# An overwritten full-height matmul in front of own-key scores and projections in layer 1's attention

## The chip, the cores and the metric

One NeuronCore of one Trainium2 chip runs the whole program. Its engines are TensorE (PE in the rows; its weight loads are PEld), VectorE (DVE), ScalarE (ACT), GpSimd (POOL) and SyncE, which issues the DMAs. Each engine has its own instruction stream and takes it in order; semaphores order the engines against each other. The metric is the device time of one execution in microseconds, as the median of several.

## The reference

A stack of four layers works on x of shape (8, 256, 128): 8 batches of 256 tokens. Each layer adds a gated attention and a gated FFN to x. The change touches the attention of layer 1 alone, which is this (text has 64 keys per batch, x has 256):

```python
q = x @ Wq.T
k = jnp.concatenate([x_text @ Wk.T, x @ Wk.T], axis=1)
v = jnp.concatenate([x_text @ Wv.T, x @ Wv.T], axis=1)
...                                   # 16 heads of 8 channels
scores = jnp.einsum('bhnd,bhkd->bhnk', q, k) / jnp.sqrt(jnp.float32(d))
first = jnp.tanh(gate) * jnp.ones_like(scores[..., :1])
rest = jax.nn.softmax(scores[..., 1:], axis=-1)
attn = jnp.concatenate([first, rest], axis=-1)
out = jnp.einsum('bhnk,bhkd->bhnd', attn, v)
...                                   # to bfloat16 and back, layer norm
return out @ Wp.T + bp
```

The x that goes in is layer-normalised. Layers 0 and 2 have attention over the 64 text keys only, layer 3 has its own function.

## The kernel before, in words

The program is a sequence of stages: `setup`, then `attention` and `ffn` for layers 0, 1 and 2, `attention3` and `ffn` for layer 3, and `store`. Within a stage each engine has a function that emits its stream; all of them walk the same list of steps, and each takes the steps in which it has a part. Layer 1's attention is `attention(pr, 1, own_keys=True, ...)`. Only this call has own keys.

Its 16 heads are worked on in NG = 4 groups of 4 heads. A head's 8 channels are spread over 32 partitions (hi and lo parts of a float32 beside each other), so that one group fills the 128 partitions. The 8 batches are worked on one after the other, and within a batch the 4 groups. A batch and group has these steps:

- `proj` (L543 to L545): q and k of the group, six matmuls of 128 rows and 256 columns into `b_proj`. ScalarE (L705) and VectorE (L830) bring them to SBUF in two parts.
- `scores` (L559 and L566), NS = 5 of them. Step 0 is against the text keys, with all 4 heads at once (128 rows). Steps 1 to 4 are against the own keys, one head each: two matmuls on a strip of 32 rows. Each step fills a bank of two in turn, `b_sc`, and VectorE reduces it to row maxima (L842, L844).
- `maxima` (L579): the maxima are turned on TensorE; ScalarE and VectorE (L712, L865, L867) make of them and of q the operand `mt`.
- `weights` (L594 and L604), again 5: the transposed scores less the maximum. Step 0 has 128 rows, steps 1 to 4 have 32 rows, on the strip of head i. ScalarE takes the exponential (L718) from one of two banks, `b_st`.
- `pv` (L631), 5 steps for every two groups: 8 matmuls each, 128 rows by 32 columns, of the exponentials with the values.
- per batch: `turn` (L526) transposes the normalised x, `values` (L612) projects v, `o_turn` (L648), `on_turn` (L654) and `y` (L660) turn, normalise and project the output.

The order of the steps is written out by hand in `order(b)`. While the weights of group g are computed, the scores of group g+2 and the projection of group g+3 are issued. A group begins with the first score step of group g+2, the projection of g+3 and the maxima of g+1; then `mixed` interleaves the weights of g, the other score steps of g+2 and the value products: weights 0, scores 1, pv, weights 1, scores 2, pv, weights 2, scores 3, pv (in every other group), weights 3, scores 4, weights 4. In the prediction k counts these rounds from 0. Weights k lie on the row strip of head k-1 and scores k+1 on that of head k, so the two are on different strips for k of 1 to 3.

What holds TensorE in these steps: an own-key score step waits until VectorE has reduced the step two before it (`sc_taken`, from the helper `need`), a weights step until ScalarE has taken the one two before (`exp_done`), a projection until x has been turned (`xt_lo`) and the projection before it has been taken (`qk_split`).

Of the kernel before, what the change touches and what calls it, by code (L numbers as in the profile page):

```python
# [23 lines left out]
P = 128  # L24
# [27 lines left out]
def need(eng, sem, value):  # L52

    if isinstance(value, int) and value <= 0:
        return
    eng.wait_ge(sem, value)
# [117 lines left out]
def attention(pr, layer, own_keys, masked, biased, scale, extra=None):  # L174
# [8 lines left out]
    with nc.cleanup_on_exit(), ExitStack() as scope:  # L183
        def sb(name, shape, dt=F32):
            return scope.enter_context(nc.sbuf_tensor(f"{n}_{name}", shape, dt))

        wf = sb("wf", [P, 4, D]) if gated else None
        wx = sb("wx", [P, 4, NG * P], F32R)
# [70 lines left out]
        b_proj, b_turn, b_sc, b_st, b_mt, b_o = (pr.bank[0], pr.bank[1], pr.bank[2:4], pr.bank[4:6], pr.bank[6], pr.bank[7])  # L259
# [65 lines left out]
        with nc.Block() as block:  # L325
# [152 lines left out]
            def _(pe):  # L478
# [5 lines left out]
                if biased:  # L484

                    pe.wait_ge(sem["prep_dve"], 3)
                    for i in range(2):
                        for g in range(NG):
                            last = pe.matmul(b_sc[1][:, i * NG + g:i * NG + g + 1], bias_x[0:1, i, g * P:(g + 1) * P], ones1[0:1, 0:1],
                                             start=True, stop=True)  # L490
# [9 lines left out]
                for h, bank in enumerate((b_proj, b_turn)):  # L500
                    if biased:
                        pe.matmul(bank[:], ones1[:], bias_row[0:1, 2:3, :].to_broadcast([1, 4, D]), start=True, stop=False, skip_group_check=True)
                    for e in range(4):
                        last = pe.matmul(bank[:, e * D:(e + 1) * D], pr.ctx_t2[:, 4 * h + e].rearrange("p a s -> p (a s)"), w[2],
                                         start=not biased, stop=True, skip_group_check=True)
                    last.then_inc(sem["prep_pe"], 1)
                if gated:

                    for h in range(2):
                        pe.wait_ge(sem["prep_dve"], DVE_READY)  # L510
                        for e in range(4):
                            last = pe.matmul(b_sc[h][:, e * D:(e + 1) * D], pr.ctx_t2[:, 4 * h + e, 0, 0:1].to_broadcast([P, P]), wvg[:],
                                             start=True, stop=True, skip_group_check=True)
# [2 lines left out]
                pe.wait_ge(sem["prep_act"], ACT_READY)  # L516
                pe.wait_ge(sem["prep_pool"], POOL_READY)

                def turn(b):
                    pe.wait_ge(sem["xn_ready"], b + 1)  # L520
                    if own_keys:
                        need(pe, sem["v_ready"], b)
                    need(pe, sem["x_done"], b - 2)
                    need(pe, sem["xt_lo"], b)
                    for t in range(2):
                        last = pe.transpose(b_turn[:, t * P:(t + 1) * P], xn[:, t], pr.id())  # L526
                    last.then_inc(sem["xn_turned"], 1)
# [9 lines left out]
                def proj(b, g):  # L537
                    pe.wait_ge(sem["xt_lo"], b + 1)
                    need(pe, sem["qk_split"], b * NG + g)
                    cols = slice(g * P, (g + 1) * P)  # L540
                    for i in range(2 if own_keys else 1):
                        o = b_proj[:, i * S:(i + 1) * S]
                        pe.matmul(o, wx[:, 2 * i, cols], xt_hi[:], start=True, stop=False)  # L543
                        pe.matmul(o, wx[:, 2 * i, cols], xt_lo[:], start=False, stop=False)
                        last = pe.matmul(o, wx[:, 2 * i + 1, cols], xt_hi[:], start=False, stop=True)  # L545
                    last.then_inc(sem["proj_done"], 1)

                def scores(b, g, i):
                    at = g * NS
                    need(pe, sem["sc_taken"], b * U + (at + i - 1))  # L550
                    o = b_sc[(at + i) % 2]
                    if i == 0:
                        pe.wait_ge(sem["qk_split"], b * NG + g + 1)
                        pe.wait_ge(sem["kc_ready"], b * NG + g + 1)
                        if masked:
                            pe.wait_ge(sem["mk_split"], b + 1)
                        for t in range(2):
                            ts = slice(t * P, (t + 1) * P)
                            last = pe.matmul(o[:, t * S:(t + 1) * S], q[:, g, ts], kc[:, g], start=True, stop=not masked)  # L559
                            if masked:  # L560
                                last = pe.matmul(o[:, t * S:(t + 1) * S], msk[:, ts], i2[:, 0:S2].unsqueeze(1).to_broadcast([P, GH, S2]),
                                                 start=False, stop=True)
                    else:
                        rows = slice(32 * (i - 1), 32 * i)
                        for t in range(2):
                            last = pe.matmul(o[:, t * S:(t + 1) * S], q[rows, g, t * P:(t + 1) * P], k[rows, g], start=True, stop=True)  # L566
                    last.then_inc(sem["sc_done"], 1)
# [89 lines left out]
                def y(b):  # L657
                    pe.wait_ge(sem["o2t_ready"], b + 1)
                    for t in range(2):
                        last = pe.matmul(b_turn[:, t * P:(t + 1) * P], o2t[:, t * P:(t + 1) * P], w[3], start=True, stop=True)  # L660
                    last.then_inc(sem["y_done"], 1)

                passes(pe, {"turn": turn, "mask": mask, "proj": proj, "scores": scores, "maxima": maxima, "weights": weights,
                            "values": values, "pv": pv, "o_turn": o_turn, "on_turn": on_turn, "y": y})

# [1209 lines left out]
```

## Time and profile before

| | us |
|---|---|
| median of 3 runs | 1292.36 |
| lowest and highest | 1283.95, 1293.24 |
| the profiled execution | 1285.64 |
| its span, first to last instruction | 1283.9 |
| TensorE busy in the span | 977.4 |
| VectorE busy | 771.4 |
| ScalarE busy | 571.7 |
| GpSimd busy | 393.6 |

The profile is of one execution. The mean granted clock of TensorE over it was 0.842 of full speed. In the profile's rows a matmul's duration is the time from its start to its modelled end; matmuls overlap, so what one costs is read from the distance between starts.

### The profile page before, as it was taken

What the parts mean: (1) busy time and instruction counts of PE and PEld (TensorE: products, weight loads), DVE (VectorE), ACT (ScalarE), POOL (GpSimd) and SP (SyncE); (2) the same over time, 40 slices, a digit from 0 to 9 for tenths busy, and PEclk for the clock granted to TensorE, in tenths of its full rate; (3) what the DMA queues carried; (4) which work ended last, traced back from release to release, by engine and by line L of the source; (5) the groups of instructions that cost most, each with busy time, mean ns of one, the idle gap of its engine ahead of it and who ended that gap; (6) DMA issues with size and microseconds to landing.
All of it is one profiled execution on the core that took longest, in us unless ns stands there. A gap on an engine that the chain in (4) does not pass through costs nothing. (4 is left out here: it accounts for less than half of the span.)

```text
span 1283.9 us, 17163 instructions
## 1 busy us (share of the span) xinstructions
PE 977.4 (76%) x5366; PEld 731.0 (57%) x5366; DVE 771.4 (60%) x1924; ACT 571.7 (45%) x1101; POOL 393.6 (31%) x519
## 2 busy tenths in 40 slices
PE   2797576698888888488888888478867578883766
PEld 2575354566566665266666666357745357772544
DVE  3687565566766777366666656356765414545674
ACT  1575242355555555155555544156634133321553
POOL 2432002122323232146565656333310132210321
PEclk9899677667777778689999999689978679996887
DMA  4000000000000000000000000100000200000001
GB/s 117 1 2 2 1 1 19 1 18 18 18 18 18 18 9 10 1 1 1 1 1 1 1 1 1 36 1 2 2 19 1 64 2 1 1 1 1 1 1 33
DMA packets 25607, 14.12 MB, mean 11 GB/s; under 512 B 10776, under 2 KB 25007, under 8 KB 25391
## 3 DMA queue, kind: packets, MB, share of 16 engines
q1 hardware_dynamic: 25518, 13.03, 3.8%
q8 instruction: 45, 0.74, 0.2%
q14 instruction: 44, 0.35, 0.1%
HBM read 11.98 MB, written 1.05 MB: 10 GB/s over the span
## 5 line engine op out<-in xcount | busy, mean ns | idle before, releaser
L1470 POOL TENSOR_TENSOR L1f_h<-L1f_h,L1f_gb 128x512 f32<-128x512 f32 (+1 forms) x96 | 152.2, 1588 | 116.5 <-DVE L1f_h L1760 96.7
L718 ACT ACTIVATE L_pt<-bank 128x512 f32<-128x512 f32 x224 | 131.3, 597 | 60.8 <-PE bank L604 56.9
L705 ACT ACTIVATE L_part<-bank,L_bias_ca,const 128x256 fp32r<-128x256 f32 x128 | 68.9, 563 | 111.9 <-PE bank L545 111.9
L406 POOL TENSOR_TENSOR L_kc<-L_kc_all,const 128x256 fp32r<-128x256 f32 x96 | 59.0, 618 | 179.7 <-PE bank L604 127.1
L1760 DVE TENSOR_TENSOR L1f_h<-L1f_a,bank 128x512 f32<-128x512 f32 (+1 forms) x96 | 65.4, 682 | 69.9 <-ACT L1f_a L1600 69.3
L1600 ACT ACTIVATE L1f_a<-bank 128x512 f32<-128x512 f32 (+1 forms) x96 | 57.3, 597 | 111.9 <-PE bank L1525 111.8
L1768 DVE TENSOR_TENSOR L1f_h_lo<-L1f_h,L1f_h_hi 128x512 fp32r<-128x512 f32 (+1 forms) x96 | 88.2, 919 | 11.1 <-ACT L1f_h_hi L1613 11.1
L844 DVE TENSOR_REDUCE L_ms<-bank 128x2 f32<-128x512 f32 x128 | 84.5, 687 | 17.0 <-PE bank L566 16.7
L566 PE MATMUL bank<-L_k,L_q 32*128 32x256 f32 x256 | 73.4, 397 | 12.2 <-DVE L_ms L844 8.9
L830 DVE SCALAR_TENSOR_TENSOR L_q<-bank,L_bias_c,L_part 128x256 fp32r<-128x256 f32 x96 | 46.2, 481 | 58.9 <-ACT L_part L705 57.7
L842 DVE TENSOR_REDUCE L_mc<-bank 128x8 f32<-128x512 f32 (+1 forms) x96 | 65.4, 682 | 24.2 <-PE bank L559 14.8
L1523 PE MATMUL bank<-L1f_xt_hi,big_hi 128*128 128x512 f32 (+1 forms) x192 | 77.6, 404 | 0.0
L1524 PE MATMUL bank<-L1f_xt_lo,big_hi 128*128 128x512 f32 (+1 forms) x192 | 76.6, 399 | 0.0
L1525 PE MATMUL bank<-L1f_xt_hi,big_lo 128*128 128x512 f32 (+1 forms) x192 | 76.4, 398 | 0.0
L604 PEld LDWEIGHTS bank<-L_mt,L_k 32*128 32x128 f32 x256 | 45.2, 228 | 43.9 <-ACT L_pt L718 25.3
L604 PE MATMUL bank<-L_mt,L_k 32*128 32x256 f32 x256 | 66.9, 365 | 2.1 <-ACT L_pt L718 2.1
L543 PE MATMUL bank<-L_xt_hi,L_wx 128*128 128x256 f32 x128 | 46.8, 366 | 24.5 <-DVE L_xt_lo L817 18.6
L1545 PE MATMUL bank<-L1f_h_hi,big_hi 128*128 128x512 f32 (+1 forms) x96 | 41.4, 431 | 30.0 <-DVE L1f_h_lo L1768 29.7
L559 PE MATMUL bank<-L_kc,L_q 128*128 128x256 f32 x192 | 56.9, 362 | 8.5 <-DVE L_msk L824 5.2
L1613 ACT CAST L1f_h_hi<-L1f_h 128x512 fp32r<-128x512 f32 (+1 forms) x96 | 59.0, 615 | 2.1 <-POOL L1f_h L1470 2.1
L566 PEld LDWEIGHTS bank<-L_k,L_q 32*128 32x128 f32 x256 | 45.0, 235 | 24.3 <-DVE L_ms L844 13.9
L631 PE MATMUL bank<-L_pt,L_vs 128*32 128x256 f32 x512 | 48.8, 465 | 0.0
(405 smaller groups left out, 2608.9 us busy)
## 6 DMA issues: line engine op xcount, KB each, us to landing
L_raw<-in_L_ffn_w_dram SPq DMA_DIRECT2D x8, 176.0 KB, 2.3
L_raw<-in_L_ffn_v_dram SPq DMA_DIRECT2D x8, 176.0 KB, 2.5
const<-in_const_dram SPq DMA_DIRECT2D x1, 1036.0 KB, 5.0
x<-in_x_dram SPq DMA_DIRECT2D x2, 512.0 KB
L_raw<-in_L_ffn_w_dram SPq DMA_DIRECT2D x8, 128.0 KB, 2.6
L_mask<-in_mask_Bx1xSxS_ff_dram SPq DMA_DIRECT2D x2, 512.0 KB
out_dram<-x SPq DMA_DIRECT2D x2, 512.0 KB
L_raw<-in_L_ffn_w_dram SPq DMA_DIRECT2D x8, 48.0 KB, 2.5
```

The lines of the kernel that those rows point to most:

```text
L566: last = pe.matmul(o[:, t * S:(t + 1) * S], q[rows, g, t * P:(t + 1) * P], k[rows, g], start=True, stop=True)
L604: last = pe.matmul(op, k[rows, g, kt * P:(kt + 1) * P], mt[rows, g % 2], start=True, stop=True)
L705: last = act.activation(part[:, i].bitcast(F32R), b_proj[:, i * S:(i + 1) * S], ACT.Identity, bias=bias_ca[:, i, g:g + 1], scale=pr.c("ak" ...
L718: act.activation(pt[:, g // 2, (g % 2) * NS + i], b_st[(g * NS + i) % 2][:], ACT.Exp, scale=scale).then_inc(sem["exp_done"], 1)
L842: dve.tensor_reduce(mc[:].rearrange("p t j -> p (t j)"), by_head[:, :, start:], AX_X, ALU.max).then_inc(sem["sc_taken"], 1)
L844: dve.tensor_reduce(ms[:, :, i - 1], bank.rearrange("p (t s) -> p t s", s=S), AX_X, ALU.max).then_inc(sem["sc_taken"], 1)
L1470: pool.tensor_tensor(h[0:m, r], h[0:m, r], gb[0:m, gate_slot(c)], ALU.mult).then_inc(sem["h_done"], 1)
L1523: pe.matmul(bank[0:m], hi[:, at:at + m], xh, start=True, stop=False)
L1524: pe.matmul(bank[0:m], hi[:, at:at + m], xl, start=False, stop=False)
L1525: last = pe.matmul(bank[0:m], lo[:, at:at + m], xh, start=False, stop=True)
L1760: dve.tensor_tensor(h[0:m, r], a[0:m, r], b_u[c % NS][0:m], ALU.mult).then_inc(sem["half_done"], 1)
L1768: dve.tensor_tensor(h_lo[0:m, r], h[0:m, r], h_hi[0:m, r].bitcast(F32), ALU.subtract).then_inc(sem["lo_done"], 1)
```

## The change

In TensorE's stream of the attention a helper is added which issues one matmul: the first 128 columns of `wx[:, 0]` as weights (128 rows, 128 columns) and `wx[:, 1]` as the moving operand (512 columns), start and stop set, into a whole bank. It is called with `b_proj` after the waits of a projection and before its first matmul, and with the score bank `o` in front of the two matmuls of each own-key score step. The matmuls that follow write the same columns with start set, so the result is overwritten. Both calls are made only where the layer has own keys, which is layer 1: 32 projections and 128 score steps. No semaphore, wait or other engine is touched.

```diff
@@ -516,6 +516,10 @@
                 pe.wait_ge(sem["prep_act"], ACT_READY)
                 pe.wait_ge(sem["prep_pool"], POOL_READY)
 
+                def keep_clock(bank):
+
+                    pe.matmul(bank[:], wx[:, 0, 0:P], wx[:, 1], start=True, stop=True)
+
                 def turn(b):
                     pe.wait_ge(sem["xn_ready"], b + 1)
                     if own_keys:
@@ -538,6 +542,8 @@
                     pe.wait_ge(sem["xt_lo"], b + 1)
                     need(pe, sem["qk_split"], b * NG + g)
                     cols = slice(g * P, (g + 1) * P)
+                    if own_keys:
+                        keep_clock(b_proj)
                     for i in range(2 if own_keys else 1):
                         o = b_proj[:, i * S:(i + 1) * S]
                         pe.matmul(o, wx[:, 2 * i, cols], xt_hi[:], start=True, stop=False)
@@ -561,6 +567,7 @@
                                 last = pe.matmul(o[:, t * S:(t + 1) * S], msk[:, ts], i2[:, 0:S2].unsqueeze(1).to_broadcast([P, GH, S2]),
                                                  start=False, stop=True)
                     else:
+                        keep_clock(o)
                         rows = slice(32 * (i - 1), 32 * i)
                         for t in range(2):
                             last = pe.matmul(o[:, t * S:(t + 1) * S], q[rows, g, t * P:(t + 1) * P], k[rows, g], start=True, stop=True)
```

## Rows read from the trace of the kernel before

**Rows 1.** The page: span, and TensorE's granted clock in 40 slices.

```profile
span 1283.9 us, 17163 instructions
...
PEclk9899677667777778689999999689978679996887
```

**Rows 2.** Windows: busy PE, PEld, DVE, ACT, POOL; PEclk, DMA share, GB/s.

```profile
225.00:530.00 305.00, 257.85 (x1677) 178.42 (x1677) 200.76 (x426) 155.01 (x309) 79.00 (x168) 0.73 0.05 13
397.10:433.40 36.30, 31.98 (x209) 22.29 (x209) 25.02 (x54) 18.95 (x38) 9.85 (x21) 0.73 0.06 15
399.00:405.00 6.00, 5.75 (x35) 3.13 (x34) 4.05 (x8) 3.71 (x8) 1.81 (x8) 0.50 0.00 0
497.00:503.00 6.00, 5.47 (x52) 3.35 (x51) 4.47 (x9) 3.58 (x8) 0.00 (x0) 1.00 0.01 4
600.00:700.00 100.00, 85.66 (x367) 63.38 (x366) 65.96 (x111) 53.50 (x97) 57.59 (x38) 1.00 0.00 1
```

**Rows 3.** Waits of TensorE, 300 to 510 us: total, times, longest.

```profile
PE bank L654 <- DVE L_on L895: 7.8, 6, 1.3
PE bank L566 <- DVE L_ms L844: 6.4, 12, 0.9
PE bank L543 <- DVE L_xt_lo L817: 6.1, 5, 1.3
PE bank L612 <- DVE x L902: 3.5, 6, 0.6
```

**Rows 4.** Timeline of TensorE, 2.4 GHz: start, us, line, shapes, count.

```profile
496.88 0.28 PE L543 MATMUL bank<-L_xt_hi,L_wx 128*128 128x256 f32 x1
...
497.72 0.48 PE L594 MATMUL bank<-L_mt,L_kc 128*128 128x256 f32 x2
498.13 0.50 PE L566 MATMUL bank<-L_k,L_q 32*128 32x256 f32 x2
...
499.13 0.38 PE L604 MATMUL bank<-L_mt,L_k 32*128 32x256 f32 x1
499.14 0.38 PE L566 MATMUL bank<-L_k,L_q 32*128 32x256 f32 x1
...
499.56 0.64 PE L631 MATMUL bank<-L_pt,L_vs 128*32 128x256 f32 x8
500.13 0.49 PE L604 MATMUL bank<-L_mt,L_k 32*128 32x256 f32 x2
501.16 0.51 PE L566 MATMUL bank<-L_k,L_q 32*128 32x256 f32 x2 [0.53 <-DVE L_ms L844]
501.59 0.64 PE L631 MATMUL bank<-L_pt,L_vs 128*32 128x256 f32 x8
```

**Rows 5.** Timeline of TensorE, one group at 1.2 GHz.

```profile
397.10 0.58 PE L543 MATMUL bank<-L_xt_hi,L_wx 128*128 128x256 f32 x1 [0.77 <-DVE L_xt_lo L817]
...
398.82 0.78 PE L594 MATMUL bank<-L_mt,L_kc 128*128 128x256 f32 x2
399.53 0.79 PE L566 MATMUL bank<-L_k,L_q 32*128 32x256 f32 x2
...
401.27 0.58 PE L566 MATMUL bank<-L_k,L_q 32*128 32x256 f32 x1
...
401.99 1.08 PE L631 MATMUL bank<-L_pt,L_vs 128*32 128x256 f32 x8
...
405.20 1.11 PE L648 MATMUL bank<-const,L_ot 128*128 128x128 f32 x4
```

**Rows 6.** Timeline of TensorE in the FFN of layer 1.

```profile
600.00 0.39 PE L1524 MATMUL bank<-L1f_xt_lo,big_hi 128*128 128x512 f32 x1
...
600.90 0.39 PE L1525 MATMUL bank<-L1f_xt_hi,big_lo 128*128 128x512 f32 x1
```

**Rows 7.** Timeline of the weight loads, end of the group of rows 4.

```profile
502.40 0.30 PEld L604 LDWEIGHTS bank<-L_mt,L_k 32*128 32x128 f32 x2
502.83 0.30 PEld L559 LDWEIGHTS bank<-L_kc,L_q 128*128 128x128 f32 x2
```

## The prediction, made before the result was known

> **What bounds the kernel now.** I began with the page's slices: of a span of 1283.9 us, TensorE's granted clock sags in slices 7 to 16 [rows 1]. The windows place that sag: the attention of layer 1 fills about 225 to 530 us, at a mean granted clock of 0.73. The clock has two levels, 1.2 and 2.4 GHz (0.5 and 1.0 in the rows), so TensorE has the upper one for (0.73 - 0.5) / 0.5 = 0.46 of the time. One batch in the steady part, 397.10 to 433.40 us, takes 36.3 us at the same 0.73, and TensorE is busy for 31.98 of them. The layer's FFN, whose matmuls are full-height and 512 columns wide, stays at 1.00 [rows 2].
>
> Then the waits of TensorE in the attention: four releasers, at most 7.8 us each in 210 us [rows 3]; their sum is 23.8 us, about 4 us for each of the 5.8 batches in it. Three of them (17.4 us) are the chain between batches: output normalised, normalised x turned, x written; only 6.4 us wait for the row maxima of the own keys (L844). The bound is thus TensorE's own sequence, at a clock that is low half of the time, and not VectorE.
>
> The last view is the order of matmuls in one group at each clock [rows 4, 5]. One group ran at 1.00 and one at 0.50 [rows 2]. At 2.4 GHz, with three value products (L631), it is 5.95 us from the first projection at 496.88 to the next group's load at 502.83 [rows 4, 7]. At 1.2 GHz, with two, it runs from 397.10 to 405.20, 8.10 us. One L631 step at 2.4 GHz takes 0.57 us (499.56 to 500.13), so like for like it is 5.38 against 8.10: 2.7 us a group, 10.9 us a batch (the first score step and the batch's own few matmuls left out, so a little low). A batch wholly at one clock follows: with T at 2.4 and T + 10.9 at 1.2, and 0.54 x 36.3 = 19.6 us spent at 1.2, T = 31.2 fits (19.6 / 42.1 = 0.47 of the work at 1.2; 31.2 + 0.47 x 10.9 = 36.3). So **31.2 us a batch at 2.4 GHz, 42.1 at 1.2**. The clock alone has at most 36.3 - 31.2 = 5.1 us a batch to give back.
>
> What matters beside this in rows 4: the 32-row matmuls of the weights step (L604) and of the score step (L566) lie in different row groups and start together (499.13 and 499.14). The two steps, four matmuls, leave TensorE at 499.56: 0.43 us for both. One such step alone also takes 0.43 us (501.16 to 501.59). The loop's order lets k = 1 and k = 3 of each group run as such pairs, 8 in a batch. At 1.2 GHz the pair takes 0.72 us (401.27 to 401.99) [rows 5].
>
> **The change, part by part.** It removes nothing and adds 20 matmuls of 128 rows and 512 columns to a batch, with their weight loads: 4 in front of projections, 16 in front of own-key score steps. It adds no wait, and no instruction on any other engine. Each added matmul stands behind the wait for the bank it overwrites, so it can't fill that wait: it begins when the real matmul would have begun.
>
> In front of a projection its neighbours are full-height too, and the row for a 128x512 matmul among its like is the pitch of the FFN: 600.00 to 600.90 is four of them, 0.225 us [rows 6]. Four of these are 0.9 us a batch at 2.4 GHz. At 1.2 GHz it is twice the stream, 0.43, so 1.7.
>
> In front of the first own-key step (k = 0) it follows L594, full-height again, and the switch to 32 rows is paid already. Again 0.225 or 0.43 each: 0.9 or 1.7 a batch.
>
> In front of the other three it stands between L604 and L566. It uses all rows, so the pair can't run together. What a full-height stream of 512 columns costs between other shapes is best seen in L594 x2 (twice 256 columns): 497.72 to 498.13, 0.41 us at 2.4 GHz [rows 4], and 398.82 to 399.53, 0.71 at 1.2 [rows 5]. A pair becomes 0.43 + 0.41 + 0.43 = 1.27 us where it was 0.43: plus 0.84, of which half is the lost overlap. For k = 1 and 3 that is 8 x 0.84 = 6.7 us a batch. At k = 2 the score step is often alone already because it waits for L844: 500.13 to 501.59 was 1.46 us with 0.53 us of that wait, and would be 1.27 without it; where nothing waits it is 0.86 and becomes 1.27. Between -0.2 and +0.4, I take +0.2: 0.8 a batch. At 1.2 GHz a pair becomes 0.72 + 0.71 + 0.72, plus 1.43, or 11.4 for eight, and k = 2 about 1.2 each (nothing waits there, so less than a pair's 1.43), 4.8.
>
> A batch wholly at 2.4 GHz: 31.2 + 0.9 + 0.9 + 6.7 + 0.8 = 40.5 us. Of the 4 us of waits a slower TensorE should find some gone, since VectorE and ScalarE are further ahead; the chain between batches stays. I take 1.5 off: **39 us at 2.4 GHz**. Wholly at 1.2: 42.1 + 1.7 + 1.7 + 11.4 + 4.8 = **61.7 us**.
>
> The other engines are no cost: VectorE was busy 25.02 of 36.3 us in the batch [rows 2]. The work that waits behind the later score steps (the reduce L844, then the maxima) is needed a whole group later.
>
> **The clock after the change.** It should rise. The rows show 1.0 where full-height, wide matmuls run back to back [rows 2, 6], and 0.50 through 399 to 405, in which 32-row steps fill much of the time [rows 5]; the change puts 10,240 full-height columns into each batch. But it also stretches the parts between them, and the waits between batches (1.3 us is the longest) remain. The ends are the old share of 0.46 and 1. I take 0.7, a little short of the middle, because the stretches of k = 1 to 3 now last longer and still hold mostly 32-row or 32-column work. Then a batch takes 1 / (0.7 / 39 + 0.3 / 61.7) = 43.8 us, plus 7.5. With the share at 1 it is 39, plus 2.7; at 0.46 it is 1 / (0.46 / 39 + 0.54 / 61.7) = 48.7, plus 12.4.
>
> The first two groups of scores run before the loop with no partner, and the first batch is short, so I count 7.7 batches, not 8: plus 58, plus 21 and plus 95 us. Against the profiled execution (span 1283.9 us, 1285.64 us in all) the first is 1344; that execution lies at the low end of the three times and 7 us under their median. I give a little back for what waits may still hide and take 1342.
>
> **A rule against this reading.** The row: two 32-row loads (L604) are done 0.30 us after 502.40, and the next full-height load (L559) starts only at 502.83 [rows 7]. The load port was free for 0.13 us and nothing was fetched: a full-height load isn't taken ahead of 32-row work here. The Trainium skill, TensorE: Matmul & The Clock Gate, section "Step-by-step: what each phase is for", says that the queue pulls a weight load ahead also when it goes to the array's background buffer. By that rule the added load would lie hidden behind L604; this trace doesn't show it for this order of shapes.
>
> **The rivals.**
> 1. **Weight loads hidden, waits absorb.** If the added matmul costs its pitch alone everywhere, and the pairs keep their overlap, a batch at 2.4 GHz throughout is 31.2 + 20 x 0.225 = 35.7 us, minus 0.6 from now, -5 us in all. If 2 of the 4 us of waits take up the delay as well it is 33.7, minus 2.6, -20 us: **1266**, faster. It decides at k = 1 and 3: below 34.5 us a batch the kernel gains over 1%. For it speaks that 4 us of waits exist; against it the start times [rows 4, 7], and that one array can't stream a full-height matmul beside 32-row ones. The mechanism that I weighed against the page above is this one. 13 in 100, over half of it within 1%.
> 2. **The clock goes to 2.4 GHz throughout.** Plus 21 us, **1307**. For it: the FFN at 1.00 [rows 2]. Against: the waits between batches stay. 17 in 100.
> 3. **The clock doesn't rise**, because between the added matmuls TensorE now spends longer in 32-row work. Plus 95 us, **1381**. For it: groups with the same kinds of matmul stood at 0.50 from 399 to 405 us [rows 2]. 17 in 100.
> 4. **The change does nothing**, because the results are overwritten and the additions are somehow free. No row shows a free matmul. 2 in 100.
>
> **How the numbers follow.** The forecast (plus 30 to plus 80 us, share 0.55 to 0.9) has 51 in 100. The predicted time is 1342. The range leaves out the first rival and the far end of the third: 1295 to 1388. About 1% is what a measurement of this kernel can tell from no change, here 13 us. Faster by over 1%: the first rival's far part, 0.06. Within 1%: its near part, the fourth and the low edge of the second, 0.12. Slower: 0.82.
>
> **What would show it.** After the change, in one steady batch: 20 more full-height matmuls on the new line; the granted clock of the attention above 0.73, near 0.85; no L604 and L566 that start together at k = 1 to 3, but 0.8 to 0.9 us from the first L604 to L566 at 2.4 GHz; a batch of 42 to 46 us; fewer waits for L844. The forecast is wrong if pairs still start together, if the batch at 2.4 GHz takes under 36 us, or if the clock stays at 0.73 (then rival 3). Layers 0, 2 and 3 and the FFNs should keep their lengths to a few us.

## The result and the profile after

| | before | after |
|---|---|---|
| median | 1288.15 us (4 runs) | 1357.61 us (4 runs) |
| lowest and highest | 1277.4, 1293.24 | 1343.58, 1360.57 |
| ratio to before, 95% interval | | 1.0529, 1.0422 to 1.0636 |
| the profiled execution | 1285.64 | 1360.57 |

The change makes the kernel 5.3% slower, about 69 us. The profiled execution after is the slowest of its four: its mean granted clock is 0.840, that of the other three 0.845 to 0.859. The page of the kernel after gives its span and the granted clock in 40 slices:

```profile
span 1358.5 us, 17483 instructions
...
PEclk9798776577878787757999999967996978997788
```

Slices 7 to 18 (counted from 0) are the attention of layer 1 now, with the clock between 5 and 8 tenths. Line numbers move by 6 or 7: L521 is the added matmul, L573 the own-key scores (L566 before), L611 the weights step (L604), L638 the value products (L631), L549 to L551 the projection.

Where the 74.6 us between the two spans lie is read from the first matmul of one line in each stage: the value projection of batch 0 and the first matmul of the FFN that follows. Each row gives the count, min/median/max duration in ns, and the first and last start in us. Before:

```profile
L612 PE MATMUL bank<-L_wf,L_xt_raw x32: 275/399/582, 248.4 to 496.5; 128*128 128x128 f32 x32
```

```profile
L1523 PE MATMUL bank<-L1f_xt_hi,big_hi x192: 387/393/774, 546.5 to 804.6; 128*128 128x512 f32 x128, 128*96 128x512 f32 x64
```

After:

```profile
L619 PE MATMUL bank<-L_wf,L_xt_raw x32: 275/421/582, 254.5 to 562.5; 128*128 128x128 f32 x32
```

```profile
L1530 PE MATMUL bank<-L1f_xt_hi,big_hi x192: 387/393/774, 626.0 to 882.7; 128*128 128x512 f32 x128, 128*96 128x512 f32 x64
```

From batch 0's value projection to the FFN it was 546.5 - 248.4 = 298.1 us and is 626.0 - 254.5 = 371.5, 73.4 more. The scores and projections ahead of the loop take 6.1 more. From there to the end it was 1283.9 - 546.5 = 737.4 and is 732.5, 4.9 less. The whole loss is in the stage that was changed.

Windows of the kernel after: five steady batches (from the first projection matmul of one batch to that of the fifth after it), and two short stretches, one at each clock. Columns as in [rows 2].

```profile
308.53:532.58 224.05, 207.92 (x1141) 137.35 (x1140) 123.60 (x266) 96.50 (x190) 49.39 (x105) 0.79 0.05 13
486.00:493.00 7.00, 7.00 (x49) 4.39 (x48) 4.06 (x8) 4.34 (x9) 2.75 (x11) 1.00 0.01 4
506.00:522.00 16.00, 15.42 (x60) 10.31 (x59) 6.63 (x14) 5.01 (x10) 1.34 (x2) 0.50 0.00 2
```

The same five batches before:

```profile
289.13:470.00 180.87, 158.49 (x1041) 110.00 (x1041) 124.73 (x266) 94.82 (x190) 49.30 (x105) 0.73 0.06 16
```

A batch took 180.87 / 5 = 36.2 us and takes 224.05 / 5 = 44.8, forecast 43.8. TensorE is at 2.4 GHz for (0.79 - 0.5) / 0.5 = 0.58 of it, before 0.46. So the clock did rise, and the kernel lost all the same. VectorE has the same work (124.73 and 123.60 us) in a longer time.

The five steady batches hold 43.2 of the 73.4 us. Ahead of them, from batch 0's value projection, it is 13.3 us more (40.73 and 54.03); behind them, up to the FFN, 16.9 more (76.50 and 93.42). In that last stretch the granted clock was 0.73 and is 0.67.

A group at 2.4 GHz after, which answers to [rows 4]:

```profile
485.31 0.50 PE L521 MATMUL bank<-L_wx 128*128 128x512 f32 x1 [1.08 <-DVE L_xt_lo L824]
...
488.12 0.50 PE L611 MATMUL bank<-L_mt,L_k 32*128 32x256 f32 x2
488.55 0.51 PE L521 MATMUL bank<-L_wx 128*128 128x512 f32 x1
488.99 0.50 PE L573 MATMUL bank<-L_k,L_q 32*128 32x256 f32 x2
489.42 0.64 PE L638 MATMUL bank<-L_pt,L_vs 128*32 128x256 f32 x8
489.98 0.49 PE L611 MATMUL bank<-L_mt,L_k 32*128 32x256 f32 x2
...
491.17 0.39 PE L611 MATMUL bank<-L_mt,L_k 32*128 32x256 f32 x2
...
492.60 0.66 PE L655 MATMUL bank<-const,L_ot 128*128 128x128 f32 x4
```

And at 1.2 GHz, which answers to [rows 5]:

```profile
505.45 0.63 PE L521 MATMUL bank<-L_wx 128*128 128x512 f32 x1
...
510.31 0.79 PE L611 MATMUL bank<-L_mt,L_k 32*128 32x256 f32 x2
511.03 0.80 PE L521 MATMUL bank<-L_wx 128*128 128x512 f32 x1
...
512.48 1.08 PE L638 MATMUL bank<-L_pt,L_vs 128*32 128x256 f32 x8
513.49 0.79 PE L611 MATMUL bank<-L_mt,L_k 32*128 32x256 f32 x2
...
515.53 0.62 PE L611 MATMUL bank<-L_mt,L_k 32*128 32x256 f32 x2
...
517.96 1.22 PE L667 MATMUL bank<-L_wf,L_o2t 128*128 128x128 f32 x4
```

In both the weights step L611, the added L521 and the score step L573 follow each other; no two of these steps start together. At 2.4 GHz that is 0.43 + 0.44 + 0.43 us (starts at 488.12, 488.55, 488.99, 489.42), and a round with its value product lasts 489.98 - 488.12 = 1.86 where it lasted 1.00 (499.13 to 500.13 in [rows 4]). At 1.2 GHz it is 513.49 - 510.31 = 3.18 us. The score step's row at 511.75 is left out above.

The waits of TensorE in the five batches, after and then before (total us, times, longest):

```profile
PE bank L661 <- DVE L_on L902: 6.5, 5, 1.3
PE bank L521 <- DVE L_xt_lo L824: 6.2, 6, 1.1
PE bank L619 <- DVE x L909: 2.9, 5, 0.6
PE bank L521 <- DVE L_ms L851: 1.5, 3, 0.5
```

```profile
PE bank L543 <- DVE L_xt_lo L817: 7.0, 6, 1.3
PE bank L654 <- DVE L_on L895: 6.5, 5, 1.3
PE bank L566 <- DVE L_ms L844: 5.4, 10, 0.9
PE bank L612 <- DVE x L902: 2.9, 5, 0.6
```

The list before has one more, 1.3 us for ScalarE's exponentials (L_pt), left out above. The three waits of the chain between batches are nearly as they were (16.4 us and 15.6). Those for the own keys' maxima (L_ms) fell from 5.4 to 1.5 us, 0.8 us a batch.

### The profile page after: what moved, and what is told of

It is laid out like the page before. It is cut to its first block and busy times, and to the rows that moved or that the text cites. A ratio compares the mean times of both kernels' runs of the same rounds, so it can differ in the third digit from the quotient of the medians.

```text
span 1358.5 us, 17483 instructions
## 1 busy us (share of the span) xinstructions
PE 1067.4 (79%) x5526; PEld 779.2 (57%) x5526; DVE 768.2 (57%) x1924; ACT 574.1 (42%) x1101; POOL 392.7 (29%) x519
## 3 DMA queue, kind: packets, MB, share of 16 engines
HBM read 11.98 MB, written 1.05 MB: 10 GB/s over the span
## 5 line engine op out<-in xcount | busy, mean ns | idle before, releaser
L521 PE MATMUL bank<-L_wx 128*128 128x512 f32 x160 | 90.6, 566 | 15.3 <-DVE L_xt_lo L824 8.1
L573 PE MATMUL bank<-L_k,L_q 32*128 32x256 f32 x256 | 74.9, 377 | 0.0
L573 PEld LDWEIGHTS bank<-L_k,L_q 32*128 32x128 f32 x256 | 45.2, 220 | 39.2 <-issue 39.2
L611 PE MATMUL bank<-L_mt,L_k 32*128 32x256 f32 x256 | 66.2, 349 | 0.7 <-ACT L_pt L725 0.7
L611 PEld LDWEIGHTS bank<-L_mt,L_k 32*128 32x128 f32 x256 | 44.9, 221 | 37.9 <-issue 30.9
L521 PEld LDWEIGHTS bank<-L_wx 128*128 128x128 f32 x160 | 37.4, 234 | 33.5 <-DVE L_xt_lo L824 10.1
```

Of the source, the lines that this page charges most:

```text
L521: pe.matmul(bank[:], wx[:, 0, 0:P], wx[:, 1], start=True, stop=True)
L611: last = pe.matmul(op, k[rows, g, kt * P:(kt + 1) * P], mt[rows, g % 2], start=True, stop=True)
```

## The experiments

Each kernel below is compared with the kernel before as it ran beside it on the same chip. The diffs of 1 to 5 are against the kernel after, that of 6 is against the kernel before with `keep_clock` added; all are cut to the lines that matter. Times are medians of several executions; windows and shares are of the one that was profiled. Each window is of five steady batches of that kernel; share is the part of the time at 2.4 GHz, (PEclk - 0.5) / 0.5.

**1. Only where both neighbours are full-height.**

```diff
                     else:
-                        keep_clock(o)
+                        if i == 1:
+                            keep_clock(o)
```

> Keeps 8 of the 20 added matmuls of a batch: in front of the projections and of the first own-key score step, where both neighbours are full-height. Theory (a full-height matmul among its like costs its stream, the rest of the loss is broken pairs): 1.8 us a batch at 2.4 GHz and 3.4 at 1.2, with a clock share of about 0.6 in place of 0.46, so 1 / (0.6 / 33 + 0.4 / 45.5) = 37.1 us a batch against 36.3: +6 us over the kernel before, between -10 and +20. Rival (each added matmul costs the same wherever it stands): 8/20 of the change's 69 us, +28. L604 and L566 still start together.

Measured: 1280.76 us against 1288.27, ratio 0.9938 (0.9906 to 0.9970).

```profile
289.60:467.11 177.51, 156.35 (x1081) 107.92 (x1080) 123.02 (x265) 94.73 (x190) 49.20 (x105) 0.82 0.06 16
```

35.5 us a batch at a share of 0.64. Eight added matmuls of a batch buy more clock than they cost. The rival of an equal cost everywhere (+28) is out; my own forecast (+6) was inside its range, on the wrong side of zero.

**2. Only in the middle of the pairs.**

```diff
-                    if own_keys:
-                        keep_clock(b_proj)
...
-                        keep_clock(o)
+                        if i > 1:
+                            keep_clock(o)
```

> Keeps the other 12 of 20: in front of own-key score steps 2 to 4, between a 32-row weights step and a 32-row score step. Theory: all of the loss sits here, 7.5 us a batch at 2.4 GHz and 16 at 1.2, less 1.5 of waits, at a clock share near 0.5: about 45 us a batch, +60 us over the kernel before (+45 to +80). Rival (same cost everywhere): 12/20 of 69, +41.

Measured: 1335.13 us, ratio 1.0376 (1.0306 to 1.0447), 47 us slower.

```profile
303.99:512.80 208.81, 194.08 (x1101) 130.35 (x1101) 122.34 (x266) 96.40 (x190) 49.18 (x105) 0.81 0.05 14
```

41.8 us a batch at a share of 0.62. These 12 places alone lose 47 of the change's 69 us. By size alone 47 us is as near the rival's 41 as my 60, so this run needs the first beside it: 8 places gave -7.5 us and 12 gave +47. The two do not sum to 69. Put on top of the 12, the same 8 cost 22 us (1335.13 to 1357.61; the intervals of the two ratios just meet). That is about what their own 1.8 to 3.4 us a batch come to with no gain on the clock, and the share is 0.58 with all 20. So "all of the loss sits here" was too strong; why the 8 pay for themselves alone and not beside the 12 was not tried.

**3. The same 20 matmuls, 12 of them one step earlier**, ahead of the pair in place of inside it.

```diff
-                        keep_clock(o)
+                        if i == 1:
+                            keep_clock(o)
...
                     else:
+                        if i < NS - 1:
+                            keep_clock(o)
                         rows = slice(32 * (i - 1), 32 * i)
                         for kt in range(2):
                             op = o[:, kt * S:(kt + 1) * S]
```

> All 20 matmuls of a batch, but the 12 stand in front of weights steps 1 to 3 (bank b_st) in place of score steps 2 to 4, so the 32-row steps of a pair stay neighbours and can start together. Theory: each costs its own 0.41 (2.4 GHz) or 0.71 us (1.2), and the lost overlap of 0.43 or 0.72 is not paid: about 42 us a batch, +44 us over the kernel before (+25 to +55), that is 15 to 40 us faster than the change. Rival (overlap of pairs is worth nothing, the streamed columns are the cost): no difference from the change, +69.

Measured: 1280.60 us, ratio 0.9959 (0.9924 to 0.9993). That is 77 us faster than the change, with the same number, size and height of added matmuls (the kernel before took 1288.27 us beside this one and 1288.15 beside the change). The rival, no difference from the change, is out.

```profile
292.68:468.42 175.74, 159.58 (x1141) 102.94 (x1140) 120.19 (x266) 94.22 (x190) 49.50 (x105) 0.93 0.06 17
```

```profile
405.85 0.50 PE L521 MATMUL bank<-L_wx 128*128 128x512 f32 x1
406.28 0.39 PE L614 MATMUL bank<-L_mt,L_k 32*128 32x256 f32 x1
406.29 0.38 PE L574 MATMUL bank<-L_k,L_q 32*128 32x256 f32 x1
...
406.71 0.64 PE L641 MATMUL bank<-L_pt,L_vs 128*32 128x256 f32 x8
407.28 0.50 PE L521 MATMUL bank<-L_wx 128*128 128x512 f32 x1
```

The weights step (here L614) and the score step (L574) start together again, at 406.28 and 406.29, and both are through at 406.71, 0.43 us later. The added matmul costs its own 0.43 (405.85 to 406.28), and the round is 1.43 us. The change's round is 1.86: the 0.43 between them is the lost overlap alone. My theory had the direction against the change right and the size far wrong: 35.1 us a batch and not 42, and 8 us faster than the kernel before where I had 44 slower. Two things show. The share is 0.86, against 0.58 in the change. And the added matmul now stands ahead of the wait for the maxima, so it runs in it: of the waits of TensorE only the three between batches are left (7.9 us for L_xt_lo, 6.5 for L_on, 2.9 for x), and the 5.4 us for L_ms of the kernel before are gone, 1.1 us a batch.

Between this kernel and the change lie 9.7 us a batch. Twelve overlaps of 0.43 us are 5.2 of them at 2.4 GHz, and twelve of 0.72 are 8.6 at 1.2 (an estimate from the pairs of both traces); the rest goes with the higher clock. The 77 us are both together, and no run separates them.

**4. The 20 places with 32 columns in place of 512.**

```diff
-                    pe.matmul(bank[:], wx[:, 0, 0:P], wx[:, 1], start=True, stop=True)
+                    pe.matmul(bank[:, 0:32], wx[:, 0, 0:P], wx[:, 1, 0:32], start=True, stop=True)
```

> All 20 matmuls at their places in the change, but 32 columns wide in place of 512, so next to nothing is streamed and the pairs are still broken. Theory (switching between shapes and the lost overlap are the cost, and the wide stream buys clock): the pairs still cost about 0.63 us each at 2.4 GHz and 1.1 at 1.2, and the clock share drops to 0.3 or so: about 47 us a batch, +50 to +90 us over the kernel before, no better than the change. Rival (the 512 streamed columns are the cost): at most +15 us.

Measured: 1377.73 us, ratio 1.0704 (1.0637 to 1.0771), 89 us slower than the kernel before, at the upper edge of what was expected, and 20 us slower than the change with a sixteenth of its added columns.

```profile
305.26:550.69 245.43, 232.22 (x1142) 168.63 (x1142) 127.46 (x266) 96.91 (x190) 48.54 (x105) 0.58 0.04 12
```

```profile
406.22 0.79 PE L611 MATMUL bank<-L_mt,L_k 32*128 32x256 f32 x2
406.94 0.40 PE L521 MATMUL bank<-L_wx 128*128 128x32 f32 x1
407.26 0.79 PE L573 MATMUL bank<-L_k,L_q 32*128 32x256 f32 x2
407.99 1.08 PE L638 MATMUL bank<-L_pt,L_vs 128*32 128x256 f32 x8
```

49.1 us a batch at a share of 0.16, where I had 47 and 0.3. Here (1.2 GHz) the weights step takes 0.72, the narrow matmul 0.32 and the score step 0.73 us, where the pair took 0.72 in all. That is 1.05 us more (406.22 to 407.99, less 0.72); the full-width matmul of the change adds 1.44 there. The rival that the streamed columns are the cost is out: most of what a full-height matmul costs between the two steps stays without its columns, and the clock falls below that of the kernel before.

**5. The 20 places, 512 columns wide but 32 rows high.**

```diff
-                def keep_clock(bank):
+                def keep_clock(bank, strip=0):
 
-                    pe.matmul(bank[:], wx[:, 0, 0:P], wx[:, 1], start=True, stop=True)
+                    rows = slice(32 * strip, 32 * strip + 32)
+                    pe.matmul(bank[:], wx[rows, 0, 0:P], wx[rows, 1], start=True, stop=True)
...
-                        keep_clock(o)
+                        keep_clock(o, i - 1)
```

> All 20 places of the change, 512 columns wide, but 32 rows high, on the strip of the score step that follows. Theory (height decides for the clock; broken pairs decide for the rest): the clock share stays at 0.46 or falls, and the added matmul can stream beside the weights step on its own strip, so a batch is 42 to 47 us: +45 to +85 us over the kernel before, at a clock in the attention of 0.73 or less. Rival (width alone holds the clock): PEclk of the attention at 0.78 or more and at most +35 us.

Measured: 1396.00 us, ratio 1.0840 (1.0774 to 1.0905), 109 us slower than before and outside my range.

```profile
307.78:562.60 254.82, 241.61 (x1141) 158.41 (x1140) 126.66 (x265) 96.86 (x190) 49.08 (x105) 0.50 0.04 11
```

```profile
403.35 0.58 PE L612 MATMUL bank<-L_mt,L_k 32*128 32x256 f32 x1
403.36 0.79 PE L522 MATMUL bank<-L_wx 32*128 32x512 f32 x1
...
404.50 1.08 PE L639 MATMUL bank<-L_pt,L_vs 128*32 128x256 f32 x8
```

The granted clock is 0.50 over all five batches: not once in 255 us does it rise, with TensorE busy for 241.61 of 254.82 us, 95%. The added matmul does start beside the weights step (403.35 and 403.36), so a pair with it takes 1.15 us (403.35 to 404.50) at 1.2 GHz and not 2.17 as in the change (510.31 to 512.48); the batch is still 51.0 us. Neither a busy TensorE nor width without height (this kernel, share 0) holds the clock, and height without width (kernel 4, share 0.16) hardly does; the same 20 places with both gave 0.58. My range for a batch (42 to 47) took the share of before as its upper end and did not allow for zero.

**6. In the waits only** (`fill_waits` in the expectations). A helper waits until the projection bank has been read (no wait for that shows in the trace) and issues matmuls into the bank ahead of the wait proper.

```diff
+                def fill(taken, times):
+
+                    if own_keys and taken > 0:
+                        pe.wait_ge(sem["qk_split"], taken)
+                        for _ in range(times):
+                            keep_clock(b_proj)
...
                 def proj(b, g):
+                    if g == 0:
+                        fill(b * NG, 4)
                     pe.wait_ge(sem["xt_lo"], b + 1)
...
                 def values(b):
                     if own_keys:
+                        fill(b * NG + NG - 1, 3)
                         need(pe, sem["x_done"], b - 1)
...
                 def on_turn(b):
+                    fill(min((b + 2) * NG + 2, B * NG), 4)
                     pe.wait_ge(on_ready, b + 1)
```

> None of the 20 places of the change. Instead 11 full-height 512-column matmuls a batch into the projection bank, put ahead of the waits in which TensorE stands still between batches: 4 before it waits for the normalised output (L_on), 3 before the wait for x (L612 of before), 4 before the wait for xt_lo at the first projection of a batch. Theory (the clock falls after thin stretches and waits, and the clock is worth about 14 us between a batch at 1.2 and one at 2.4 GHz): the matmuls run in idle time, 0.7 to 0.9 us in waits of 0.6 to 1.3 us, and the clock share rises to about 0.7: about 33 to 35 us a batch, -20 us against the kernel before (-35 to 0). Rival (what fills a wait delays the chain behind it as much as it gives): 0 to +20 us.

Measured: 1274.41 us against 1286.96, ratio 0.9872 (0.9822 to 0.9921).

```profile
290.68:458.40 167.72, 155.68 (x1096) 108.67 (x1096) 121.09 (x266) 95.18 (x190) 49.25 (x105) 0.86 0.06 17
```

```profile
PE bank L579 <- DVE L_ms L859: 10.3, 19, 0.7
PE bank L556 <- DVE L_xt_lo L832: 1.9, 5, 0.4
PE bank L669 <- DVE L_on L910: 0.2, 1, 0.2
```

33.5 us a batch at a share of 0.72. The rival (0 to +20 us) is out. The expectation's 14 us between a batch at either clock stands on no row here; the prediction had 10.9. The three waits between batches fell from 16.4 us to 2.1, and the wait for L_ms (L579 here is its score step) rose from 5.4 to 10.3: with TensorE faster, VectorE's row maxima are the next thing late.

**7. Waits and full-height neighbours**, kernels 6 and 1 together (`fill_full` in the expectations).

> The 11 matmuls ahead of waits and the 8 between full-height neighbours (in front of projections and of the first own-key score step). Theory: the two gains on the clock add, share 0.85 or more, at 1.8 us a batch for the 8: 32 to 33.5 us a batch, -28 us against before (-40 to -12). Rival (the 8 bring all that the clock can give): no better than the 8 alone, -8 us.

Measured: 1267.15 us, ratio 0.9841 (0.9796 to 0.9886), 20 us faster than before and 90 us faster than the change, the fastest of all. It beats both kernels of this case, and its interval lies below that of kernel 1, so the rival (the 8 bring all that the clock can give) is out. Its advantage over kernel 6 is not settled (the intervals overlap).

```profile
301.13:466.40 165.27, 155.44 (x1137) 107.51 (x1135) 121.72 (x266) 95.18 (x190) 49.17 (x105) 0.93 0.06 18
```

33.1 us a batch at a share of 0.86.

**8. How much of it.** Kernel 7 with one more matmul a group ahead of the last pair:

> As fill_full, with one more matmul a group ahead of the pair of weights step 3 and score step 4, 4 a batch, at 0.43 us each: it fills the stretch where 32-row steps follow each other without a value product. Theory: share above 0.9, but 1.7 us dearer: within 8 us of fill_full either way.

Measured: 1283.01 us, ratio 0.9969 (0.9933 to 1.0005); 16 us slower than kernel 7, twice what I allowed. The clock did not rise (PEclk 0.92 over the five batches, 293.30 to 466.18, against 0.93; over the whole executions 0.867 to 0.880, against 0.873 to 0.884), so the 0.43 us each were paid for nothing. Kernel 7 with 6, 5 and 6 matmuls in the waits:

> fill_full with 6, 5 and 6 matmuls ahead of the three waits in place of 4, 3 and 4. In fill_full 0.39 us of the wait for xt_lo is still left and the other two are gone. Theory: a batch holds 6 more matmuls of 0.225 us at 2.4 GHz, of which 0.4 us fits into idle time, and the clock share has little left to gain (0.87): 0 to +9 us against fill_full. Rival (the share goes to 1): -5 to -12 us against fill_full.

Measured: 1272.11 us against 1284.51, ratio 0.9910 (0.9878 to 0.9942).

```profile
292.61:465.95 173.34, 167.21 (x1166) 118.56 (x1165) 120.99 (x266) 95.29 (x190) 49.67 (x105) 0.88 0.06 17
```

34.7 us a batch at a share of 0.76, but the profiled execution is not typical: its mean granted clock is 0.867, and that of the other nine 0.878 to 0.883, where kernel 7 had 0.873 to 0.884. So the clock was as a rule neither lower nor higher than in kernel 7. By the ratios this kernel is 0.7% slower than kernel 7, with intervals that touch. Six matmuls at 0.225 us are 1.35 us a batch, and kernel 7 had 0.66 us a batch of these waits left (2.4 us for L_xt_lo and 0.9 for L_on in five batches; the expectation had the second as gone): by this estimate the real matmuls are put off by some 5 us in eight batches, and the medians are 5 us apart. Last, kernel 7 without the matmul in front of the first own-key step:

> fill_full without the 4 matmuls a batch in front of the first own-key score step. Theory: 0.9 us a batch less work, a share between that of fill_waits (0.72) and fill_full (0.87): within 6 us of fill_full either way, so 0.98 to 0.99 of before.

Measured: 1273.37 us, ratio 0.9900 (0.9854 to 0.9946), 6.2 us from kernel 7 and so at the very edge of what was expected. It is not told apart from kernels 6 and 7.

## Why the prediction was right, step by step

**The mechanism.** The steps that it rested on show. Lost overlap and own cost were put at 0.84 us for a pair at 2.4 GHz and 1.43 at 1.2; measured are 1.86 - 1.00 = 0.86 and 3.18 - 1.74 = 1.44 (1.74 is from 401.27 in [rows 5] to the next weights step 403.00 of the kernel before's trace). Experiment 3 shows the halves apart: 0.43 us for the matmul, 0.43 for the overlap. In front of a projection the added matmul was forecast at 0.225 and 0.43 us; in the trace after it takes 0.23 at 2.4 GHz (493.33 to the projection's 493.56), 0.34 right behind a wait (485.31 to 485.65), and 0.43 at 1.2 GHz (505.45 to 505.88).

**A group.** By the terms of the prediction a group with two value products would be 5.38 + 0.45 + 2 x 0.84 + 0.2 = 7.71 us at 2.4 GHz, from the projection to L655; it is 492.60 - 485.31 = 7.29. At 1.2 GHz it would be 8.10 + 0.86 + 2.86 + 1.2 = 13.02 and is 517.96 - 505.45 = 12.51. Both are 0.4 to 0.5 us too high, about 2 us a batch. The rounds k = 2 and 3 hold the difference. Two more rows of the kernel before at 1.2 GHz are needed:

```profile
403.00 0.58 PE L604 MATMUL bank<-L_mt,L_k 32*128 32x256 f32 x1
...
403.61 0.62 PE L604 MATMUL bank<-L_mt,L_k 32*128 32x256 f32 x2
```

At 2.4 GHz the round k = 2 went from 1.46 us (500.13 to 501.59), 0.53 of them a wait, to 1.19 (489.98 to 491.17): 0.27 less, where the prediction had 0.2 more. At 1.2 GHz it went from 0.61 (403.00 to 403.61) to 2.04 (513.49 to 515.53), 1.43 more and not 1.2: it was a pair there like the others. What made that sum too high is the end of the group: from weights step 3 on it took 1.59 (403.61 to 405.20, with a wait of 0.25 for ScalarE in it) and takes 2.43 (515.53 to 517.96), 0.84 more and not 1.43.

**The waits.** The prediction took 1.5 us a batch off at 2.4 GHz. All waits of TensorE in the five batches fell from 23.1 to 17.1 us, 1.2 a batch.

**The clock share**, the other estimated term, was off the other way: 0.7 forecast, 0.58 measured (in the profiled execution; the other three had a higher clock). By the prediction's own formula, 39 and 61.7 us at the measured share give 1 / (0.58 / 39 + 0.42 / 61.7) = 46.1. So the share alone was worth 2.3 us a batch, and terms that were 1.3 too high took part of that back: 43.8 forecast against 44.8 measured is nearer than either term, and that is luck. One batch of the trace after did run at the forecast share (399.45 to 441.30, PEclk 0.85, so 0.70). It took 41.85 us and not 43.8, which shows the 2 us by themselves.

**The total.** Forecast was +58 us on 7.5 us a batch; measured is +73.4 in the stage and +6.1 ahead of it, less 4.9 later. 8.6 us over 7.7 batches are 66. The other 7 lie outside the steady batches, where the last stretch lost clock (0.73 to 0.67). The added matmuls ahead of the loop, which make the 6.1 us, were counted at nothing.

**The rivals.** The first (weight loads hidden, overlap kept) is out: the added matmul takes a full 0.43 us of the round, and no score step starts beside a weights step (the nearest starts of two such matmuls in the layer lie 0.116 us apart). The weight loads of two added matmuls of the group at 2.4 GHz are these, the first behind full-height work (k = 0), the second behind the 32-row weights step (k = 1):

```profile
486.69 0.19 PEld L521 LDWEIGHTS bank<-L_wx 128*128 128x128 f32 x1
...
488.55 0.19 PEld L521 LDWEIGHTS bank<-L_wx 128*128 128x128 f32 x1
```

The first load starts 0.12 us ahead of its matmul (486.81), the second with its matmul (488.55). It is so in the whole layer: behind full-height L601 (weights step 0) the load leads by 0.11 to 0.21 us in all 30 cases, behind L611 by 0.002 us at most in all 90. The reading of the Trainium skill (TensorE: Matmul & The Clock Gate, "Step-by-step: what each phase is for") by which the load might be fetched ahead into the background buffer does not show here for a full-height load behind 32-row work: by it the added matmul would take its stream alone, 0.225 us, and it takes 0.44 (488.55 to 488.99). The second (a share of 1) and the third (no rise) bracket what happened.

**What the prediction missed** is not what the clock has to give. It put that at 5.1 us a batch at most. Kernel 6 gained 2.7 us a batch by going from a share of 0.46 to 0.72; in proportion the whole way to 1 would be 5.6 (an estimate). What it didn't look for is a cheaper way to buy the clock: it noted that each added matmul stands behind its wait and so can't fill it, and did not ask what the same matmul costs ahead of a wait. Kernel 6 shows a net gain there, with the three waits between batches down by 2.9 us a batch; two of my later expectations (1 and 3) were too slow as well.

## What to carry to other kernels

A matmul added only to hold TensorE's clock has two prices: its own stream, and what it separates. Look for 32-row matmuls on different row strips that start together in the trace and never put a full-height one between them; here that one step of order was 77 us, lost overlap and lower clock together. Put such matmuls ahead of the waits that bound a stage, not behind them, and only about as many as the wait holds (more gained nothing here); then see what is late next, here the row maxima on VectorE.

## What was not expected of the hardware

- The same 20 matmuls a batch, in the same places and of the same width, left the granted clock at 0.50 for 255 us on end when they were 32 rows high, TensorE busy for 95% of the time (experiment 5), and gave 0.79 at full height. I had expected the old 0.73 at best, not the floor.
- The granted clock differs between executions of the same kernel on the same chip: its mean was 0.825 to 0.847 in seventeen executions of the kernel before (1298.82 us the longest, 1281.6 the shortest), and in the kernel with 25 matmuls a batch 0.867 once and 0.878 to 0.883 nine times. The traced execution can be the odd one, as it was there.
